# The last tile's steps behind its attended values: other banks, and an earlier place in the order

## The chip, the cores and the metric

One core of a Trainium2 chip runs the whole program. The metric is device time in microseconds (us); 830.11 us is the median of three runs of the kernel before.

## The reference

32 sequences of 128 tokens, 256 features, all in float32. What is computed for each sequence `x` (a "tile" below):

```python
x = x + tanh(g_xattn) * cross_attention(layernorm(x), ctx, mask)        # part "A": 16 heads of 16
y = layernorm(x)
# part "B":
q = k = rope(y) @ Wqk;  v = y @ Wv                                      # 16 heads, causal
u = layernorm(y + softmax(q k^T / 4, causal) v @ Wo; ln1)
gates = top2(softmax(u @ Wg + bg))                                      # 8 experts, two kept
m = u + sum_e gates[e] * (u @ We + be)                                  # all 8 products are computed
x = x + tanh(g_ffn) * layernorm(m; ln2)
```

## The kernel before, in words

There is no loop in the program: five Python functions write out the instruction order of five engines, and semaphores tie them together. `for r in rounds` emits, per round, two tiles; each step is called with its own tile number, `2 * r - 6` for instance, so that up to ten tiles are in flight. A step whose tile is outside 0 to 31 emits nothing (`live`). Each engine runs its own list strictly in the order written; a step that waits holds everything behind it on its engine.

TensorE (`tensor_program`, L385 to L741) makes for a tile: scores, attended values (`attend`, L561), their transposition to rows (`normalise`, L579), the transposes of the normalised values (`o_transposed`), the output product (`project_o`), the transposes of u (`u_transposed`), the gate product (`gate`), the transposes of the gates, the bias product (`expert_bias_sum`, L611) and four products of two experts each (`expert_pair`, L613, six matmuls of 512 columns through `products`, L395). `keep_busy` (L407) emits matmuls of which nobody reads the result; they only occupy TensorE.

Products are made in float32r from a high and a low part of each operand. So a transposed tile in PSUM is read by ScalarE, which writes the high part (`high_part`, L756), and then by VectorE, which subtracts it and writes the low part (`low_part`, L971); TensorE waits for the latter.

VectorE (L928 to L1251) also divides by the softmax sums (`inverse_sums` L1043, `normalise` L1051), adds the residual (`finish_b` L1069), takes mean and variance (`statistics` L952, `mean_variance` L960), applies them (`apply_u`, `apply_v`, L964), computes the gates from L1077 (`gate`, `gate_rank`, `gate_choice`, to L1107), and adds up the experts: `bias_sum` (L1122) and eight `expert_sum` (L1131) for a tile, each reading what the one before wrote. GpSimd takes the roots (`inverse_root`, L1260 and L1263), scales and shifts u (`scale_shift_u`, L1334 and L1336), and finishes the output (`finish`, L1305 to L1311). SyncE loads and stores; `y_out` is one buffer, so `finish` waits for the store before.

PSUM has eight banks. Four are `score_banks`, for the scores of one tile at a time; the table `WORK_USES` deals the other four, `work_banks`, out to everything else in a fixed turn: `work_bank(use, n)` gives the bank, and `work_last(use, n)` finds the use before it in that bank, for whose reader `take_work` makes TensorE wait. For the last tiles:

```python
    ("pair3", 1, 2, 3, (("moe", 9, 9),)),          # odd tiles: work bank 2, read by the last expert sum
    ("B_normalise", 1, 2, 2, (("B_on", 1, 1),)),   # odd tiles: the next use of work bank 2
```

After tile 31's scores (exponentials read for the last time at 791.7 us) the score banks have no further use.

Of the kernel before, what the change touches and what calls it, by code (L numbers as in the profile page):

```python
# [21 lines left out]
GROUPS = HEADS // GROUP  # L22
# [8 lines left out]
PAIR = 2  # L31
# [3 lines left out]
U_SLOTS = 2  # L35
# [100 lines left out]
def build(nc, dram, out):  # L136
    tiles = out.shape[0]
    with ExitStack() as ctx:
# [96 lines left out]
        def live(t):  # L235
            return 0 <= t < tiles

        def work_bank(use, n):

            key = (use, None) if (use, None) in WORK_AT else (use, n % PAIR)  # L240
            return work_banks[WORK_USES[WORK_AT[key]][2]]

        def work_last(use, n):

            key, pair = ((use, None), n) if (use, None) in WORK_AT else ((use, n % PAIR), n // PAIR)
            bank, behind = WORK_USES[WORK_AT[key]][2:4]
            turn = (pair + behind) * len(WORK_USES) + WORK_AT[key] - 1
            while turn >= 0:
                _, half, other_bank, behind, readers = WORK_USES[turn % len(WORK_USES)]
# [134 lines left out]

        def tensor_program(pe):  # L385
            def take_work(use, t):
                for name, value in work_last(use, t):
                    pe.wait_ge(sem[name], value)
                return work_bank(use, t)
# [237 lines left out]
            for r in rounds:  # L627
# [5 lines left out]
                if r == 0:  # L633
                    keep_busy("A_max_t", 0, 6)
                x_t(2 * r)
                project_o("B", 2 * r - 5)
# [5 lines left out]
                expert_pair(0, 2 * r - 6)  # L642
                expert_bias_sum(2 * r - 6)
                expert_pair(1, 2 * r - 6)
                expert_pair(2, 2 * r - 6)
                if r == 1:
                    keep_busy("A_v", 2, 15)
# [4 lines left out]
                rope_transposed(2 * r - 2)  # L652
                subtract_max("A", 2 * r - 1)
                normalise("B", 2 * r - 4)
                expert_pair(3, 2 * r - 6)
# [4 lines left out]
                u_transposed(2 * r - 5)  # L660
                y_transposed(2 * r - 3)
                if r == 2:
                    keep_busy("A_v", 4, 4)
# [36 lines left out]
                if r == 18:  # L700
                    keep_busy("pair1", 31, 3)
                expert_bias_sum(2 * r - 5)
                expert_pair(1, 2 * r - 5)
                if r == 0:
                    keep_busy("A_max_t", 0, 13)
# [1 line left out]
                    keep_busy("rope_t", 1, 14)  # L707
                if r == 2:
                    keep_busy("B_normalise", 1, 8)
                scores_t("A", 2 * r)  # L710
                transpose_max("A", 2 * r)
                rope_transposed(2 * r - 1)
# [1 line left out]
                expert_pair(2, 2 * r - 5)  # L714
                project_k_b(r - 1)
                expert_pair(3, 2 * r - 5)
                project_q_b(r - 1)
                if r == 17:
                    keep_busy("u_t", 30, 5)
                normalise("B", 2 * r - 3)  # L720
                u_transposed(2 * r - 4)
                if r == 1:
                    keep_busy("A_values", 2, 8)
                if r == 2:
# [6 lines left out]
                o_transposed("B", 2 * r - 3)  # L731
                project_v_a(2 * r + 1)
                normalise("A", 2 * r)
                if r == 16:
# [10 lines left out]
        def scalar_program(act):  # L745
# [112 lines left out]
            for r in rounds:  # L858
# [16 lines left out]
                keep_keys("B", r - 4)  # L875
                keep_queries("B", r - 4)
                high_part("y_t", y_t, "y_t", ("B_v_mm", 1), 2 * r - 8)
                high_part("u_t", u_t, "u_t", ("e_mm", 4), 2 * r - 10)
                raw_values("A", 2 * r - 6)
                high_part("B_o_t", o_t["B"], "B_ot", ("B_o_mm", 1), 2 * r - 9)  # L880
                max_transposed("B", 2 * r - 8)
                if r == 3:
                    split_high("Bo")
# [44 lines left out]
        def vector_program(dve):  # L928
# [212 lines left out]
            for r in rounds:  # L1141
# [46 lines left out]
                mean_variance("1", 2 * r - 6)  # L1188
                gates_low(2 * r - 7)
                maxima("A", 2 * r - 2)  # L1190
                bias_sum(2 * r - 7)
                max_parts("A", 2 * r - 2)
                expert_sum(0, 2 * r - 7)
                expert_sum(1, 2 * r - 7)
                expert_sum(2, 2 * r - 7)
# [5 lines left out]
                apply_u(2 * r - 6)  # L1201
                expert_sum(4, 2 * r - 7)
                expert_sum(5, 2 * r - 7)
                expert_sum(6, 2 * r - 7)
# [3 lines left out]
                inverse_sums("B", 2 * r - 5)  # L1208
                normalise("B", 2 * r - 5)
# [12 lines left out]
                low_part("u_t", u_t, "u_t", 2 * r - 6)  # L1222
                apply_v(2 * r - 7)
                low_part("B_o_t", o_t["B"], "B_ot", 2 * r - 5)
                mean_variance("A", 2 * r + 1)
                if r == 1:
                    split_low("Bo")
                low_part("A_o_t", o_t["A"], "A_ot", 2 * r - 2)
                gate(2 * r - 6)
                add_values("B", 2 * r - 4)  # L1230
                finish_a(2 * r - 2)
# [4 lines left out]
                finish_b(2 * r - 5)  # L1236
# [4 lines left out]
                statistics("1", 2 * r - 5)  # L1241
                gates_low(2 * r - 6)
                mean_variance("1", 2 * r - 5)
                apply_y(2 * r - 2)
                maxima("A", 2 * r - 1)
                bias_sum(2 * r - 6)
# [4 lines left out]
                apply_u(2 * r - 5)  # L1251

        def gpsimd_program(pool):
# [133 lines left out]
            for r in rounds:  # L1389
                base_a(2 * r - 5)  # L1390
                inverse_root("2", 2 * r - 10, "vn")
                context_parts(2 * r - 2)
                mask_of_tile(2 * r - 3)
                for g in range(GROUPS):
                    causal(g, 2 * r - 7)
                inverse_root("B", 2 * r - 5, "yn")
                inverse_root("A", 2 * r - 2, "xn")
                rope(2 * r - 5)
                context_parts(2 * r - 1)
                if r == 4:  # L1400
                    fold_gains()
                inverse_root("1", 2 * r - 8, "un")
                finish(2 * r - 10)
                base_b(2 * r - 7)
                scale_shift_u(2 * r - 8)
# [9 lines left out]
                inverse_root("1", 2 * r - 7, "un")  # L1415
                finish(2 * r - 9)
                scale_shift_u(2 * r - 7)
# [55 lines left out]
```

## Time and profile before

| | |
|---|---|
| median of 3 runs (lowest, highest) | 830.11 us (830.05, 830.32) |
| the profiled execution | 831.21 us |
| its span, first to last instruction | 829.5 us |
| TensorE, VectorE, ScalarE, GpSimd busy | 94%, 80%, 68%, 57% of the span |
| mean granted clock of TensorE | 0.994 |

Times in the trace count from the span's start. The profiled execution is one single run; 1.7 us of it lie outside the span. A matmul's busy time overlaps the next one's: back to back, 512 columns issue every 0.23 us but each is shown with 0.39 us. "idle" in a row is the engine's idle time just before it and what ended it.

### The profile page before, as it was taken

How to read it: one execution, taken by the hardware profiler on the slowest of the kernel's cores; microseconds unless marked ns; L12 is line 12 of the kernel's file. 1: busy time of each engine (PE TensorE's matmuls, PEld its weight loads, DVE VectorE, ACT ScalarE, POOL GpSimd, SP SyncE). 2: the span in 40 equal slices, each digit the busy share in tenths (PEclk: the TensorE clock that was granted, in tenths of full speed). 3: DMA queues.
4: the chain of work that ended last, by engine and by line, in shares of the span. 5: the costliest groups of instructions: out<-in, count | busy, mean ns of one | idle time of the engine just before them, and what ended most of it. 6: DMA issues, size and time to landing. Idle time of an engine off the chain costs nothing.

```text
span 829.5 us, 24325 instructions
## 1 busy us (share of the span) xinstructions
PE 779.7 (94%) x9515; PEld 611.9 (74%) x9515; DVE 667.5 (80%) x1908; ACT 564.4 (68%) x1268; POOL 473.0 (57%) x854
## 2 busy tenths in 40 slices
PE   8888989999999999999999999999999999999896
PEld 4465768777787787778787788778778777777663
DVE  5756668797978979797988979797988979787876
ACT  5786767777786777777776777678677777764320
POOL 8434535566665646566574646566564655555343
PEclk9999999999999999999999999999999999999999
DMA  7510000010100101010100101010010000000000
GB/s 202 159 39 16 2 17 16 8 37 9 37 8 2 37 8 36 9 36 9 29 16 2 38 8 37 8 37 9 10 35 2 9 8 8 9 8 8 8 7 20
DMA packets 33570, 20.75 MB, mean 25 GB/s; under 512 B 11672, under 2 KB 33456, under 8 KB 33456
## 3 DMA queue, kind: packets, MB, share of 16 engines
q1 hardware_dynamic: 33456, 19.19, 8.1%
q8 instruction: 76, 1.25, 0.6%
q14 instruction: 38, 0.31, 0.1%
HBM read 14.99 MB, written 4.19 MB: 23 GB/s over the span
## 4 chain that ended last, share of the span: by engine, by line
PE 56%; ACT 24%; DVE 14%; issue 4%; POOL 1%; DMA 0%; SPq 0%; DVEq 0%; POOLq 0%
PE bank L395 26%; PE bank L516 8%; PE bank L535 7%; ACT bank L776 6%; DVE neg_max_A L1022 6%; ACT bank L785 5%; DVE moe L1131 4%; ACT probs_B L826 3%; PE bank L556 3%; PE bank L585 3%; ACT probs_A L826 3%; PE bank L574 2%; PE bank L404 2%; ACT k_heads_B L809 2%; PE bank L546 1%
## 5 line engine op out<-in xcount | busy, mean ns | idle before, releaser
L1343 POOL TENSOR_SCALAR_AFFINE_SELECT probs_B<-probs_B 128x512 f32<-128x512 f32 x128 | 77.3, 640 | 184.4 <-ACT probs_B L826 184.4
L1131 DVE SCALAR_TENSOR_TENSOR moe<-bank,gates,moe 128x256 f32<-128x256 f32 x256 | 123.2, 481 | 48.2 <-PE bank L395 33.2
L785 ACT ACTIVATE bank<-mask_add 128x512 f32<-128x512 bf16 x128 | 76.6, 602 | 49.2 <-DVE neg_max_A L1022 49.2
L395 PE MATMUL bank<-w_expertsa,u_t_a 128*128 128x512 f32 x256 | 105.6, 413 | 0.1
L395 PE MATMUL bank<-w_expertsa,u_t_b 128*128 128x512 f32 x256 | 100.9, 394 | 0.0
L395 PE MATMUL bank<-w_expertsb,u_t_a 128*128 128x512 f32 x256 | 100.9, 394 | 0.0
L1022 DVE TENSOR_REDUCE neg_max_A<-bank 128x4 f32<-128x512 f32 x128 | 79.5, 684 | 11.9 <-PE bank L516 11.5
L1022 DVE TENSOR_REDUCE neg_max_B<-bank 128x4 f32<-128x512 f32 x128 | 79.3, 682 | 5.5 <-PE bank L516 5.5
L776 ACT ACTIVATE bank<-mask_add 128x512 f32<-128x512 bf16 x128 | 69.8, 626 | 0.0
L776 ACT ACTIVATE bank<-causal_add 128x512 f32<-128x512 bf16 x128 | 69.7, 623 | 0.0
L826 ACT ACTIVATE probs_A<-bank 128x512 f32<-128x512 f32 x128 | 66.1, 603 | 4.4 <-PE bank L556 2.2
L826 ACT ACTIVATE probs_B<-bank 128x512 f32<-128x512 f32 x128 | 66.2, 607 | 3.2 <-PE bank L556 1.1
L834 ACT ACTIVATE o_raw<-bank 128x512 f32<-128x512 f32 x64 | 38.5, 602 | 27.8 <-PE bank L574 27.8
L395 PEld LDWEIGHTS bank<-w_expertsa,u_t_a 128*128 128x128 f32 x256 | 49.1, 192 | 10.6 <-issue 0.4
L1260 POOL TENSOR_SCALAR var_eps<-mean_var 128x1 f32<-128x1 f32 x64 | 12.3, 192 | 77.7 <-DVE mean_var L960 75.2
L395 PEld LDWEIGHTS bank<-w_expertsa,u_t_b 128*128 128x128 f32 x256 | 48.1, 188 | 11.4
L395 PEld LDWEIGHTS bank<-w_expertsb,u_t_a 128*128 128x128 f32 x256 | 48.3, 189 | 6.7
L535 PEld LDWEIGHTS bank<-q_heads_A,k_heads_A 32*128 32x128 f32 x1024 | 31.4, 186 | 22.4 <-ACT bank L785 22.4
L809 ACT ACTIVATE k_heads_A<-bank,k_cols_A,head_rows 128x256 f32<-128x256 f32 x64 | 30.9, 565 | 23.0 <-PE bank L395 23.0
L535 PE MATMUL bank<-q_heads_A,k_heads_A 32*128 32x128 f32 x1024 | 37.5, 283 | 8.1 <-ACT bank L785 7.4
L411 PE MATMUL bank<-ident_bf 128*128 128x512 bf16 x167 | 42.7, 396 | 1.9 <-ACT k_heads_B L809 1.9
L516 PE MATMUL bank<-k_heads_A,q_heads_A 32*128 32x256 f32 x512 | 36.7, 399 | 5.8 <-ACT bank L776 4.7
(224 smaller groups left out, 2440.5 us busy)
## 6 DMA issues: line engine op xcount, KB each, us to landing
x_in<-in_x SPq DMA_DIRECT2D x32, 128.0 KB, 2.2
ctx_t<-in_ctxT SPq DMA_DIRECT2D x32, 128.0 KB, 2.2
out<-y_out SPq DMA_DIRECT2D x32, 128.0 KB, 1.7
w_stage<-in_expertsT SPq DMA_DIRECT2D x8, 256.0 KB, 4.3
mask_u<-in_masks SPq DMA_DIRECT2D x32, 32.0 KB, 2.1
w_stage<-in_in_projT SPq DMA_DIRECT2D x3, 256.0 KB, 4.8
w_stage<-in_WkT SPq DMA_DIRECT2D x1, 256.0 KB, 3.5
w_stage<-in_WvT SPq DMA_DIRECT2D x1, 256.0 KB, 3.6
```

Of the source, the lines that this page charges most:

```text
L395: done = pe.matmul(out_ap, l, r, start=n == 0, stop=n == len(terms) - 1)
L411: pe.matmul(bank[:], ident_bf[:], ident_bf[:].unsqueeze(1).to_broadcast([P, GROUP, P]), start=True, stop=True)
L516: done = pe.matmul(score_banks[g][:, c * 2 * P:(c + 1) * 2 * P], queries[strip, half, c, :], keys[strip, half, c, :, :], start=False, stop ...
L535: pe.matmul(score_banks[g][:, i * P:(i + 1) * P], keys[strip, half, c, odd, :], queries[strip, half, c, :], start=tag == "B" and i == 0, s ...
L776: act.activation(score_banks[g][:].rearrange("p (h k) -> p h k", k=P), mask[:, 0:1, :].to_broadcast([P, GROUP, P]), ACT.Copy).then_inc(sem ...
L785: act.activation(score_banks[g][:].rearrange("p (h k) -> p h k", k=P), mask_add[t % MASK_SLOTS][:, 1:2, :].to_broadcast([P, GROUP, P]), AC ...
L809: act.activation(k_heads[tag][pair % PAIR_SLOTS][:, :, c, odd, :], bank[:, c * PAIR * P:(c + 1) * PAIR * P].rearrange("p (j n) -> p j n", ...
L826: act.activation(probs[tag][:, g * GROUP:(g + 1) * GROUP, :].rearrange("p h q -> p (h q)"), score_banks[g][:], ACT.Exp, scale=SCALE).then_ ...
L834: act.activation(o_raw[:], work_bank(tag + "_values", t)[:], ACT.Copy).then_inc(sem[tag + "_or"], 1)
L1022: dve.tensor_reduce(neg_max[tag][:, g * GROUP:(g + 1) * GROUP], score_banks[g][:].rearrange("p (h k) -> p h k", k=P), AXIS_X, ALU.max, neg ...
L1131: dve.scalar_tensor_tensor(out=moe[(e + 1) % 2][:], in0=bank[:, (e % 2) * EMBED:(e % 2 + 1) * EMBED], scalar=gates[:, e:e + 1], in1=moe[e ...
L1343: pool.affine_select(out=part, in_=part, compare_op=ALU.is_ge, fill=0.0, base=0, pattern=[[0, GROUP], [1, P]], channel_multiplier=-1).then ...
```

## The change

Six uses of the last tiles are taken out of the fixed turn and given a score bank each (`LATE`: bank, and the semaphore and value for which `take_work` waits). Then steps of tiles 29 to 31 change places, in round 17 or 18 on TensorE, 18 on VectorE, 19 on GpSimd and 20 on ScalarE. Behind tile 31's `attend`, the two orders on TensorE are (k(n) is `keep_busy` with n matmuls):

```
before: bias29 pair1,2,3(29) k(5) normalise31 u_t30 o_t31 | gate30 out31 k(4) gates_t30 pair0(30) bias30 pair1,2,3(30) u_t31 k(8) gate31 pair0(31) gates_t31 k(3) bias31 pair1,2,3(31)
after:  bias29 normalise31 pair1(29) o_t31 pair2,3(29) u_t30 out31 | gate30 pair0,1(30) gates_t30 bias30 pair2(30) u_t31 pair3(30) k(6) gate31 pair0(31) gates_t31 k(3) bias31 pair1,2,3(31)
```

On VectorE, from the low part of tile 29's gates on (s0 to s7 are the expert sums, `low` the low parts, `stat` is statistics and mean):

```
before: bias29 s0-s3(29) apply_u30 s4-s7(29) stat2(29) inverse,normalise31 low_u30 apply_v29 low_o31 gate30 rank,choice30 finish_b31 stat1(31) bias30 s0-s2(30) apply_u31 s3-s7(30) stat2(30) low_u31 gate31 ...
after:  apply_u30 bias29 s0,s1(29) inverse,normalise31 s2,s3(29) low_o31 s4,s5(29) low_u30 s6,s7(29) stat2(29) apply_v29 finish_b31 stat1(31) gate30 rank,choice30 apply_u31 bias30 s0-s7(30) stat2(30) low_u31 gate31 ...
```

(In the order before, the low part of tile 30's gates lies between the two halves of stat1(31); after, it follows apply_u31.) ScalarE writes the high part of `o_t` 31 ahead of that of `u_t` 30. GpSimd does `scale_shift_u` 30 and 31 ahead of `finish` 28 and 29. `u_transposed` no longer takes its work bank's wait, for any tile; instead ScalarE waits for the products that read the old u before it writes that of tiles 30 and 31. The core of the diff:

```diff
+        LATE = {("B_normalise", tiles - 1): (0, "B_exp", GROUPS * tiles), ("B_o_t", tiles - 1): (1, "B_exp", GROUPS * tiles),
+                ("B_out", tiles - 1): (2, "B_exp", GROUPS * tiles), ("pair3", tiles - 3): (3, "B_exp", GROUPS * tiles),
+                ("u_t", tiles - 1): (0, "B_on", tiles), ("gate", tiles - 1): (1, "B_ot_b", tiles)}
         def work_bank(use, n):
+            if (use, n) in LATE:
+                return score_banks[LATE[use, n][0]]
...
-                if other_bank == bank and live(PAIR * pair):
+                if other_bank == bank and live(PAIR * pair) and (half is None or (other, PAIR * pair + half) not in LATE):
...
             def take_work(use, t):
+                if (use, t) in LATE:
+                    pe.wait_ge(sem[LATE[use, t][1]], LATE[use, t][2])
+                    return work_bank(use, t)
...
-                transpose_two(take_work("u_t", t), u[t % U_SLOTS], "u_t", t)
+                transpose_two(work_bank("u_t", t), u[t % U_SLOTS], "u_t", t)
...
-                if r == 18:
-                    keep_busy("gates_t", 30, 4)
+                if r == 18:
+                    expert_pair(0, 2 * r - 6)
+                if r == 18:
+                    expert_pair(1, 2 * r - 6)
                 transpose_gates(2 * r - 6)
...
-                    keep_busy("pair0", 31, 8)
+                    keep_busy("pair0", 31, 6)
...
+                if r == 17:
+                    normalise("B", 2 * r - 3)
                 expert_pair(1, 2 * r - 5)
...
-                if r == 17:
-                    keep_busy("u_t", 30, 5)
...
+                if use == "u_t" and t >= tiles - 2:
+                    act.wait_ge(sem[read[0]], read[1] * t)
                 act.activation(dst[0][:], work_bank(use, t)[:, 0:EMBED], ACT.Copy).then_inc(sem[name + "_a"], 1)
```

## Rows read from the trace of the kernel before

**Rows 1.** The page: busy time by engine, and one expert matmul (mean ns).
```profile
PE 779.7 (94%) x9515; PEld 611.9 (74%) x9515; DVE 667.5 (80%) x1908; ACT 564.4 (68%) x1268; POOL 473.0 (57%) x854
...
L395 PE MATMUL bank<-w_expertsa,u_t_b 128*128 128x512 f32 x256 | 100.9, 394 | 0.0
```
**Rows 2.** Busy time by stretch: PE, PEld, DVE, ACT, POOL, then PEclk, DMA share, GB/s.
```profile
800.00:802.00 2.00, 1.40 (x11) 0.93 (x8) 1.55 (x6) 0.77 (x2) 0.75 (x2) 1.00 0.00 0
...
803.00:804.00 1.00, 1.00 (x5) 0.72 (x5) 0.90 (x6) 0.25 (x2) 0.00 (x0) 0.50 0.00 0
...
806.00:807.00 1.00, 1.00 (x6) 0.80 (x5) 0.47 (x2) 0.11 (x1) 0.19 (x1) 0.94 0.00 0
```
**Rows 3.** The chain that ended last, 793 to 830 us: start, us, what.
```profile
800.56 0.43 DVE o_norm_B L1051
...
811.70 0.04 issue
...
818.01 4.22 PE bank L395 x18
```
**Rows 4.** Timeline of VectorE: start, us, engine, line, operation [idle before, releaser].
```profile
794.20 0.42 DVE L1122 TENSOR_TENSOR moe<-bank,u 128x256 f32<-128x256 f32 x1 [0.73 <-PE bank L611]
...
799.95 0.18 DVE L960 BATCH_NORM_AGGREGATE mean_var<-stats 128x2 f32<-128x6 f32 x1
800.27 0.26 DVE L1043 RECIPROCAL inv_sum_B<-bank 128x16 f32<-128x16 f32 x1
...
802.27 0.16 DVE L1077 TENSOR_TENSOR logits<-bank,gate_bias 128x8 f32<-128x8 f32 x1
...
804.10 0.23 DVE L1107 TENSOR_SCALAR gates<-chosen,gate_inv 128x24 f32<-128x24 f32 x1
804.25 0.41 DVE L1069 TENSOR_TENSOR u_n<-bank,base_B 128x256 f32<-128x256 f32 x1
...
807.54 0.42 DVE L1122 TENSOR_TENSOR moe<-bank,u 128x256 f32<-128x256 f32 x1 [0.90 <-PE bank L611]
...
809.64 0.41 DVE L964 TENSOR_SCALAR u_n<-u_n,mean_var,rstd 128x256 f32<-128x256 f32 x1
809.97 2.83 DVE L1131 SCALAR_TENSOR_TENSOR moe<-bank,gates,moe 128x256 f32<-128x256 f32 x5
...
813.39 0.39 DVE L971 TENSOR_TENSOR u_t_b<-bank,u_t_a 128x256 fp32r<-128x256 f32 x1
814.49 0.17 DVE L1077 TENSOR_TENSOR logits<-bank,gate_bias 128x8 f32<-128x8 f32 x1 [0.70 <-PE bank L595]
```
**Rows 5.** Timeline of TensorE.
```profile
793.78 0.38 PE L611 MATMUL bank<-expert_bias,gates_t 128*128 128x256 f32 x1
...
799.60 0.63 PE L585 MATMUL bank<-ident,o_raw 128*128 128x128 f32 x4 [0.16 <-DVE moe L1131]
...
803.65 1.93 PE L411 MATMUL bank<-ident_bf 128*128 128x512 bf16 x4
...
816.61 0.33 PE L604 MATMUL bank<-ident,gates 128*128 128x128 f32 x1 [0.67 <-DVE gates L1107]
...
817.63 0.39 PE L611 MATMUL bank<-expert_bias,gates_t 128*128 128x256 f32 x1
```
**Rows 6.** Timeline of ScalarE.
```profile
793.92 0.60 ACT L834 ACTIVATE o_raw<-bank 128x512 f32<-128x512 f32 x1 [0.76 <-PE bank L574]
800.49 0.38 ACT L756 ACTIVATE u_t_a<-bank 128x256 fp32r<-128x256 f32 x1 [5.97 <-PE bank L405]
```
**Rows 7.** Timeline of GpSimd.
```profile
793.18 0.55 POOL L1263 TENSOR_TENSOR rstd<-var_eps,neg_half 128x1 f32<-128x1 f32 x1
...
800.50 0.56 POOL L1263 TENSOR_TENSOR rstd<-var_eps,neg_half 128x1 f32<-128x1 f32 x1
...
810.13 0.74 POOL L1334 TENSOR_TENSOR u_n<-u_n,row_ln_w 128x256 f32<-128x256 f32 x1 [0.35 <-DVE u_n L964]
810.95 0.74 POOL L1336 TENSOR_TENSOR u<-u_n,row_ln_b 128x256 f32<-128x256 f32 x1
```

More of the change, by code:

```diff
@@ L248, in work_last @@
             while turn >= 0:
-                _, half, other_bank, behind, readers = WORK_USES[turn % len(WORK_USES)]
+                other, half, other_bank, behind, readers = WORK_USES[turn % len(WORK_USES)]
                 pair = turn // len(WORK_USES) - behind
-                if other_bank == bank and live(PAIR * pair):
+                if other_bank == bank and live(PAIR * pair) and (half is None or (other, PAIR * pair + half) not in LATE):
                     m = pair if half is None else PAIR * pair + half
@@ L635, in tensor_program @@
                 x_t(2 * r)
-                project_o("B", 2 * r - 5)
+                if r != 18:
+                    project_o("B", 2 * r - 5)
                 attend("B", 2 * r - 4)
@@ L659, in tensor_program @@
                 attend("A", 2 * r - 1)
-                u_transposed(2 * r - 5)
+                if r != 18:
+                    u_transposed(2 * r - 5)
                 y_transposed(2 * r - 3)
@@ L709, in tensor_program @@
                     keep_busy("B_normalise", 1, 8)
+                if r == 17:
+                    o_transposed("B", 2 * r - 3)
                 scores_t("A", 2 * r)
@@ L716, in tensor_program @@
                 expert_pair(3, 2 * r - 5)
+                if r == 17:
+                    u_transposed(2 * r - 4)
+                if r == 17:
+                    project_o("B", 2 * r - 3)
                 project_q_b(r - 1)
-                if r == 17:
-                    keep_busy("u_t", 30, 5)
-                normalise("B", 2 * r - 3)
-                u_transposed(2 * r - 4)
+                if r != 17:
+                    normalise("B", 2 * r - 3)
+                if r != 17:
+                    u_transposed(2 * r - 4)
                 if r == 1:
@@ L730, in tensor_program @@
                 attend("A", 2 * r)
-                o_transposed("B", 2 * r - 3)
+                if r != 17:
+                    o_transposed("B", 2 * r - 3)
                 project_v_a(2 * r + 1)
@@ L877, in scalar_program @@
                 high_part("y_t", y_t, "y_t", ("B_v_mm", 1), 2 * r - 8)
+                if r == 20:
+                    high_part("B_o_t", o_t["B"], "B_ot", ("B_o_mm", 1), 2 * r - 9)
                 high_part("u_t", u_t, "u_t", ("e_mm", 4), 2 * r - 10)
                 raw_values("A", 2 * r - 6)
-                high_part("B_o_t", o_t["B"], "B_ot", ("B_o_mm", 1), 2 * r - 9)
+                if r != 20:
+                    high_part("B_o_t", o_t["B"], "B_ot", ("B_o_mm", 1), 2 * r - 9)
                 max_transposed("B", 2 * r - 8)
@@ L1190, in vector_program @@
                 maxima("A", 2 * r - 2)
+                if r == 18:
+                    apply_u(2 * r - 6)
                 bias_sum(2 * r - 7)
@@ L1194, in vector_program @@
                 expert_sum(1, 2 * r - 7)
+                if r == 18:
+                    inverse_sums("B", 2 * r - 5)
+                if r == 18:
+                    normalise("B", 2 * r - 5)
                 expert_sum(2, 2 * r - 7)
@@ L1200, in vector_program @@
                 low_part_of_pair("rope_t", rope_t, "rope_t", 2 * r - 3)
-                apply_u(2 * r - 6)
+                if r != 18:
+                    apply_u(2 * r - 6)
+                if r == 18:
+                    low_part("B_o_t", o_t["B"], "B_ot", 2 * r - 5)
                 expert_sum(4, 2 * r - 7)
                 expert_sum(5, 2 * r - 7)
+                if r == 18:
+                    low_part("u_t", u_t, "u_t", 2 * r - 6)
                 expert_sum(6, 2 * r - 7)
@@ L1207, in vector_program @@
                 mean_variance("2", 2 * r - 7)
-                inverse_sums("B", 2 * r - 5)
-                normalise("B", 2 * r - 5)
+                if r != 18:
+                    inverse_sums("B", 2 * r - 5)
+                if r != 18:
+                    normalise("B", 2 * r - 5)
                 low_part("y_t", y_t, "y_t", 2 * r - 4)
@@ L1221, in vector_program @@
                 apply_x(2 * r)
-                low_part("u_t", u_t, "u_t", 2 * r - 6)
+                if r != 18:
+                    low_part("u_t", u_t, "u_t", 2 * r - 6)
                 apply_v(2 * r - 7)
-                low_part("B_o_t", o_t["B"], "B_ot", 2 * r - 5)
+                if r != 18:
+                    low_part("B_o_t", o_t["B"], "B_ot", 2 * r - 5)
                 mean_variance("A", 2 * r + 1)
@@ L1228, in vector_program @@
                 low_part("A_o_t", o_t["A"], "A_ot", 2 * r - 2)
+                if r == 18:
+                    finish_b(2 * r - 5)
+                if r == 18:
+                    statistics("1", 2 * r - 5)
+                if r == 18:
+                    mean_variance("1", 2 * r - 5)
                 gate(2 * r - 6)
@@ L1235, in vector_program @@
                 gate_choice(2 * r - 6)
-                finish_b(2 * r - 5)
+                if r != 18:
+                    finish_b(2 * r - 5)
                 if r == 0:
@@ L1240, in vector_program @@
                 low_part_of_pair("x_t", xn_t, "xn", 2 * r)
-                statistics("1", 2 * r - 5)
+                if r != 18:
+                    statistics("1", 2 * r - 5)
+                if r == 18:
+                    apply_u(2 * r - 5)
                 gates_low(2 * r - 6)
-                mean_variance("1", 2 * r - 5)
+                if r != 18:
+                    mean_variance("1", 2 * r - 5)
                 apply_y(2 * r - 2)
@@ L1250, in vector_program @@
                 expert_sum(2, 2 * r - 6)
-                apply_u(2 * r - 5)
+                if r != 18:
+                    apply_u(2 * r - 5)
         def gpsimd_program(pool):
@@ L1402, in gpsimd_program @@
                 inverse_root("1", 2 * r - 8, "un")
+                if r == 19:
+                    scale_shift_u(2 * r - 8)
                 finish(2 * r - 10)
                 base_b(2 * r - 7)
-                scale_shift_u(2 * r - 8)
+                if r != 19:
+                    scale_shift_u(2 * r - 8)
                 base_a(2 * r - 4)
@@ L1415, in gpsimd_program @@
                 inverse_root("1", 2 * r - 7, "un")
+                if r == 19:
+                    scale_shift_u(2 * r - 7)
                 finish(2 * r - 9)
-                scale_shift_u(2 * r - 7)
+                if r != 19:
+                    scale_shift_u(2 * r - 7)
                 if r == 1:
```

7 lines of the change are left out of this document (5 added, 2 removed).

## The prediction

> **What bounds the kernel now.** I read the busy shares first [rows 1]: TensorE is busy 94% of the span, VectorE 80%. The edits that move work act only on tiles 29 to 31, so only the last 36 us matter. The table by stage [rows 2] shows that TensorE's share there is no measure of need: from before 803 until after 806 us its granted clock is at the lower of its two levels (1.2 GHz, 0.50 in the table), and part of its busy time is filler (L411, `keep_busy`: 5, 4, 8 and 3 matmuls in this stretch). The chain of waits [rows 3] then shows what sets the end: tile 31's values normalised on VectorE, filler, tile 31's u finished by GpSimd at 811.7 [rows 7], eight fillers, the gate, and 18 expert matmuls up to 822.23. From there to the end nothing of the change acts: 7.3 us of fixed tail. So the question is at what time VectorE starts tile 31's gate (now 814.49 [rows 4]); every 0.1 us there is 0.1 us at the end, as long as TensorE has pair 0 of tile 31 ready by the time the gates are.
>
> The timelines [rows 4 to 7] show that VectorE's own queue is nearly as long as the stage. One expert sum takes 0.57 us in a chain (2.83 us for 5 [rows 4]), eight of them with the bias sum 5.0 us, and three tiles' sums are still to come at 794 us: some 15 us. Gate, ranks and choice take 2.06 us per tile (802.27 to 804.10+0.23 [rows 4]), twice here, and the rest (normalising, low parts, statistics, applying) about 6 us. That is 25 us of queue between 793.8 and the last sum's end at 823.3, which are 29.5 us. The most that any order could win is thus some 4.5 us, and it is lost by every wait that the new order puts in front of VectorE.
>
> **Part 1: the banks.** With work bank 2, tile 31's TensorE normalise had to wait for tile 29's last expert sum: it starts at 799.60 [rows 5]. In a score bank it needs only the raw values: ScalarE has them at 793.92+0.60 = 794.52 [rows 6], so it starts at 794.57, 5.0 us earlier. The `u_t` work wait that goes for all tiles costs nothing now: TensorE's order, which has waited for later VectorE work by then, implies it. By the nearest rows, bounded by the 0.04 us steps called issue [rows 3] for 32 tiles if each were exposed, it lies between 0 and -1.3 us; I take 0, since the timeline shows no gap ahead of u's transposes that it could fill. The new ScalarE wait for `e_mm` is met before the transposed tile is there (0 us) for tile 30; for tile 31 it moves the high part of u behind pair 3 of tile 30, costed below.
>
> **Part 2: tile 29's sums with tile 31's steps between them.** I follow both queues on the clock of the profiled run. TensorE: bias product of tile 29 at 793.78 as before [rows 5], normalise 794.57 to 795.04 (0.63 busy [rows 5], the last 0.16 beside the next), pair 1 of tile 29 until 796.44 (18 expert matmuls take 4.22 us [rows 3], so a pair of six 1.40; one alone is shown 0.39 long [rows 1], so its result comes 0.16 after the next could issue). VectorE: apply u of tile 30 needs the root of tile 30, 793.18+0.55 = 793.73 [rows 7], and runs at 793.83 in 0.33; bias sum 794.20 as before [rows 4]; two sums until 795.71; inverse sums and normalise (0.29 + 0.42; the reciprocal starts at 800.27 [rows 4], the product at 800.56 [rows 3]) until 796.42. TensorE's transposes of it at 796.50 with almost no stall, pair 2 until 798.16 (1.66 for both), pair 3 until 799.56. VectorE: sums 2 and 3 from 796.63 to 797.70, low part of tile 31's values, sums 4 and 5 from 798.35 to 799.42. Here comes the first new wait: next in VectorE's queue is the low part of tile 30's u, whose transposes TensorE issues only after pair 3, at 799.61. ScalarE takes 0.38 for the high part [rows 6], so the low part starts at 800.49: **1.07 us idle**, with sums 6 and 7 ready from 799.75 but queued behind. They run from 800.83 to 801.90, then statistics until 802.58.
>
> The second new wait: next is apply v of tile 29, which wants GpSimd's root of that variance. Before, tile 31's normalising and u's low part lay between. The way there took from 799.95+0.18 = 800.13 to 800.50+0.56 = 801.06 [rows 4, 7], and a crossing between the two engines 0.08 (809.64+0.41 to 810.13 [rows 4, 7]): **1.0 us idle**, apply v at 803.6. Who waits behind both: gate of tile 30, through it TensorE's gate transposes, and all of tile 30's sums. Then the moved finish B, statistics and mean of tile 31, 1.0 us (0.41 for finish B [rows 4], 0.6 for statistics and mean, as between the last sum's end at 812.80 and 813.39), so the gate starts at 804.96 rather than 802.27, and tile 30's gates are there at 804.96+2.06 = 807.02. The moved GpSimd steps are hidden: scale and shift takes 1.56 (810.13 to 811.69 [rows 7]), for tile 30 now from 794.3, and pushes the finish of tile 28 and its store 2 us back. On SyncE's queue only stores are left by then, and y_out is next rewritten after 808.9; base B of tile 31 ends by 798.8, 5 us before VectorE wants it.
>
> **Part 3: TensorE meanwhile.** Transposes of u 799.61, output product of tile 31 until 800.7, gate 800.96 to 801.42, pairs 0 and 1 of tile 30 until 804.29. Then it has nothing for 2.8 us, until 807.07. Before, these transposes issued about 805.4 (803.65 and four times 0.43), not at 804.33 when the gates were there, since four fillers at the low clock (1.93 us busy, one each 0.43 [rows 5]) stood in front. Return of the gates to the bias product: 1.02 (816.61 to 817.63 [rows 5]), so 808.10; bias sum 0.41 later at 808.51. Before it started at 807.54 [rows 4]. **The order costs 0.97 us there.** From the bias sum: 0.53 + 8 x 0.57 = about 5.0, end of tile 30's sums 813.5 against 812.80; the difference shrinks by the 0.33 of apply u, which lay among those sums (809.64 to 809.97 [rows 4]) and now runs at 806.94. Its u is there at 808.98 instead of 811.70, 2.7 us sooner; but u's low part still stands behind the statistics of tile 30 (0.59 after the last sum), at 814.10 instead of 813.39. So the earlier u is worth nothing: VectorE's queue ends last. Then 1.10 us to the gate on VectorE, as from 813.39 to 814.49 before [rows 4]: 815.20. **Sum: 815.20 - 814.49 = +0.7 us**, TensorE at full clock.
>
> The fillers: the 5 and 4 that go are under the moved work, so they are no gain of their own, and their cover, the clock, is priced here. 2.8 us without a matmul, then 0.7 more around the gates, is longer than what stood before the fall in the profiled run (1.40 us of work in 800 to 802 [rows 2]); so I expect the lower level once after 806. If it spans the gates' return, the transpose and the bias product at the half rate take some 0.1 and 0.2 more (a 512-column matmul goes from 0.23 to the fillers' 0.43 at it): +0.3. Pair 2 runs until 809.72 and pair 3, behind u's transposes, until 811.43; the sums that read them start at 811.3 and 812.4, so they have 1.4 and 0.8 us of slack, and nothing more is lost. At the least 0 (no fall); at the most, both pairs wholly cold (0.43 a matmul as the fillers [rows 5], so 2.6 a pair): 1.2 + 1.2 + 0.3 - 0.8 = 1.9. I take 0.3. The 8 fillers that become 6 stand before 814.5 and are over by 813: 0.
>
> **Total: +0.7 + 0.3 = +1.0 us.** The profiled execution took 831.21 (span 829.5 and 1.7 around it), 1.1 above the median of the runs; I put the difference on the median: 830.11 + 1.0 = 831.1.
>
> The Trainium skill (TensorE: Matmul & The Clock Gate, Terms) prices a low stretch at its length times one minus the granted share. For the stretch in rows 2, at least 3.1 us, that is 1.6 us, where the trace shows about 1.0 us of lateness on the path (gates ready 804.33, transposed 805.4). By that rule the sum here would be 0.7 + 1.6 = +2.3, 832.4.
>
> **Rivals.** (a) *The cold return.* The clock falls about when the gates come back, or stays low through both products of tile 30, and pair 3 ends after its sum wants it: +0.7 + 1.9 = +2.6, 832.7. For it: nothing fills the 2.8 us, and the filler of 4 that stood there is gone. Against it: the slack of 0.8 to 1.4 us, and the seen low stretch ended after about 3 us. It decides from 1.7 us of loss in total. The skill's rule above is this rival in other words and gives nearly its number; the chance covers both. (b) *VectorE does not stall.* If the products of tile 29 land earlier or the two waits of 1.07 and 1.03 overlap with something, the gates of tile 30 come 2.1 us sooner: 0.7 - 2.1 = -1.4, 828.7. It becomes a gain from the point where TensorE's gate transposes of tile 30 start before about 806.1, a microsecond ahead of the 807.07 above. For it: the queue has 4.5 us of air. Against: both waits follow from the written order, and neither depends on a close race. (c) *It changes nothing.* The gates' later arrival is just balanced by the filler no longer in front and by the removed work waits: 0, 830.1.
>
> **How the numbers follow.** What a measurement here can tell from no change is 0.2%, 1.7 us: faster is below 828.4, slower above 831.8. Forecast 831.1 with its own range 830.3 to 832.0: 0.48. (a) 0.23, (b) 0.15, (c) 0.14. (a) and a tenth of the forecast's spread make slower 0.29; (b) at 828.7 lies just inside the bound; if it comes, more of the 4.5 us of air than its two waits may go with it, so I count most of it as faster: 0.14 with a little unseen. The rest, 0.57, is within. Range: up to (a)'s 832.7, and down to 828.6, which keeps (b)'s own value and leaves out what may come beyond it.
>
> **What would show it.** In the new trace: TensorE's transposes of tile 31's raw values at 794.6 with the raw values as releaser; VectorE idle about 1 us before the low part of tile 30's u and again about 1 us before apply v of tile 29, released by ScalarE and GpSimd; gates of tile 30 near 807.0; TensorE idle 2.5 to 2.8 us before them, and the granted clock down once after it; tile 31's u ready near 809.0 and not waited for; its gate on VectorE at 815.2 to 815.5. I am wrong if the idle time before either of VectorE's two steps is under 0.5 us, if the clock stays low over both products of tile 30, or if anything before 793 us moves.

## The result, and the profile after

The changed kernel takes 832.58 us (median of 7 runs, 831.30 to 833.47) against 830.11 us before: ratio 1.0031, 95% interval 1.0021 to 1.0040. It is slower by 2.5 us. The forecast was +1.0 us, 831.1. 832.58 lies outside the forecast's own range (830.3 to 832.0) and above the 831.8 from which it called a result slower; it lies in the stated range only as rival (a) does, the cold return (832.7).

Of the page of the changed kernel, first the lines that answer to [rows 1]: the shares are the same, so they say nothing about the loss.

```profile
PE 777.1 (94%) x9504; PEld 610.9 (74%) x9504; DVE 667.5 (80%) x1908; ACT 564.2 (68%) x1268; POOL 472.0 (57%) x854
...
L405 PE MATMUL bank<-w_expertsa,u_t_b 128*128 128x512 f32 x256 | 101.6, 397 | 0.0
```

The two profiled executions cannot be compared by their spans (829.5 and 830.6), because the one before had lost 1.1 us earlier on, near 750 us, where TensorE's granted clock was low. These two rows are from the table by stretch of the kernel before (PE, PEld, DVE, ACT, POOL busy, then the granted clock):

```profile
745.00:750.00 5.00, 3.55 (x51) 2.81 (x43) 4.79 (x18) 0.71 (x3) 0.00 (x0) 0.81 0.00 0
750.00:755.00 5.00, 5.00 (x45) 3.97 (x44) 3.08 (x11) 2.73 (x6) 3.16 (x6) 0.85 0.01 3
```

The same stretches of the changed kernel, which issues the same work there:

```profile
745.00:750.00 5.00, 3.54 (x64) 2.61 (x61) 4.79 (x18) 1.39 (x6) 0.00 (x0) 1.00 0.00 0
750.00:755.00 5.00, 4.71 (x57) 3.92 (x56) 4.36 (x15) 2.46 (x6) 3.75 (x7) 1.00 0.01 3
```

With the clock at 1.00 there, the changed kernel starts tile 31's attended values at 791.62, the one before at 792.77. So I measure one length in every kernel, called **the stage** below: from the start of tile 31's attended values on TensorE to the start of its gate on VectorE. Before, it is 814.49 - 792.77 = 21.72 us, after 815.58 - 791.62 = 23.96: **+2.24 us**, beside 2.47 between the medians.

VectorE's timeline of the changed kernel, against [rows 4]:

```profile
793.05 0.42 DVE L1155 TENSOR_TENSOR moe<-bank,u 128x256 f32<-128x256 f32 x1
...
799.23 0.42 DVE L1004 TENSOR_TENSOR u_t_b<-bank,u_t_a 128x256 fp32r<-128x256 f32 x1 [0.96 <-ACT u_t_a L786]
...
802.34 0.41 DVE L997 TENSOR_SCALAR v_n<-moe,mean_var,rstd 128x256 f32<-128x256 f32 x1 [1.03 <-POOL rstd L1323]
...
805.49 0.23 DVE L1140 TENSOR_SCALAR gates<-chosen,gate_inv 128x24 f32<-128x24 f32 x1
...
807.55 0.42 DVE L1155 TENSOR_TENSOR moe<-bank,u 128x256 f32<-128x256 f32 x1 [0.67 <-PE bank L621]
808.08 3.43 DVE L1164 SCALAR_TENSOR_TENSOR moe<-bank,gates,moe 128x256 f32<-128x256 f32 x6
812.82 1.07 DVE L1164 SCALAR_TENSOR_TENSOR moe<-bank,gates,moe 128x256 f32<-128x256 f32 x2 [1.30 <-PE bank L405]
...
814.49 0.39 DVE L1004 TENSOR_TENSOR u_t_b<-bank,u_t_a 128x256 fp32r<-128x256 f32 x1
815.58 0.17 DVE L1110 TENSOR_TENSOR logits<-bank,gate_bias 128x8 f32<-128x8 f32 x1 [0.70 <-PE bank L605]
```

Read the brackets: 0.96 us idle until ScalarE's high part of tile 30's u, 1.03 us until GpSimd's root, and, not forecast, 1.30 us until TensorE's last expert product of tile 30, with tile 31's u ready since 807.65. TensorE's timeline shows why, against [rows 5]:

```profile
793.42 0.66 PE L595 MATMUL bank<-ident,o_raw 128*128 128x128 f32 x4 [0.40 <-ACT o_raw L864]
...
805.78 0.47 PE L614 MATMUL bank<-ident,gates 128*128 128x128 f32 x1 [2.55 <-DVE gates L1140]
806.93 0.58 PE L621 MATMUL bank<-expert_bias,gates_t 128*128 128x256 f32 x1 [0.69 <-DVE gates_t L1148]
...
809.45 0.63 PE L405 MATMUL bank<-w_expertsa,u_t_b 128*128 128x512 f32 x1
...
812.62 1.47 PE L421 MATMUL bank<-ident_bf 128*128 128x512 bf16 x6
```

It stands for 2.55 us before the gate transposes. Then an expert matmul is 0.63 long instead of 0.39, through both products behind the return of the gates. The chain of waits (start, us, what) has both products in a row, pair 2 and pair 3, each now on the path that sets the end (before, no product of tile 30 had held a sum back):

```profile
807.52 2.56 PE bank L405 x6
810.08 0.21 PE bank L414
810.29 0.21 PE bank L415
810.50 2.29 PE bank L405 x6
```

And the table by stretch, against [rows 2], shows the clock from the pause on:

```profile
804.00:805.00 1.00, 0.00 (x0) 0.00 (x0) 0.89 (x6) 0.39 (x2) 0.67 (x2) 1.00 0.00 0
805.00:806.00 1.00, 0.22 (x1) 0.18 (x1) 0.94 (x5) 0.00 (x0) 0.00 (x0) 0.74 0.00 0
806.00:807.00 1.00, 0.32 (x2) 0.07 (x1) 0.32 (x2) 0.28 (x1) 0.81 (x2) 0.50 0.00 0
...
811.00:812.00 1.00, 1.00 (x3) 0.72 (x3) 0.48 (x1) 0.00 (x0) 0.00 (x0) 0.50 0.10 34
812.00:813.00 1.00, 1.00 (x5) 0.54 (x4) 0.18 (x1) 0.13 (x1) 0.00 (x0) 0.85 0.00 0
```

By these rows the granted clock is at the lower level from about 805.5 (0.74 over that microsecond) to about 812.3 (0.85): 6.8 us, where the low stretch of the kernel before, from about 802.7 to 806.1, lasted 3.4.

### The profile page after: what moved, and what is told of

Its sections match the earlier page's. It is cut to its first block, busy times and chain, and to the rows that moved or that the text cites. A ratio compares the mean times of both kernels' runs of the same rounds, so it can differ in the third digit from the quotient of the medians.

```text
span 830.6 us, 24273 instructions
## 1 busy us (share of the span) xinstructions
PE 777.1 (94%) x9504; PEld 610.9 (74%) x9504; DVE 667.5 (80%) x1908; ACT 564.2 (68%) x1268; POOL 472.0 (57%) x854
## 4 chain that ended last, share of the span: by engine, by line
PE 55%; ACT 24%; DVE 14%; issue 4%; POOL 1%; SPq 1%; DMA 0%; DVEq 0%; POOLq 0%
PE bank L405 26%; PE bank L526 8%; PE bank L545 7%; ACT bank L806 6%; DVE neg_max_A L1055 6%; ACT bank L815 5%; DVE moe L1164 4%; ACT probs_B L856 3%; PE bank L595 3%; PE bank L566 3%; ACT probs_A L856 3%; PE bank L584 2%; PE bank L414 2%; ACT k_heads_B L839 2%; PE bank L556 1%
## 5 line engine op out<-in xcount | busy, mean ns | idle before, releaser
L421 PE MATMUL bank<-ident_bf 128*128 128x512 bf16 x156 | 39.1, 390 | 1.9 <-ACT k_heads_B L839 1.9
```

The source lines that it names most:

```text
L421: pe.matmul(bank[:], ident_bf[:], ident_bf[:].unsqueeze(1).to_broadcast([P, GROUP, P]), start=True, stop=True)
```

## The experiments

Theory 1: the loss is +0.7 us of waits in VectorE's queue plus 1.5 us of TensorE at its lower clock behind the pause that those waits make. Rivals: the clock is hidden beside VectorE; VectorE is bound by its amount of work, so waits only move; the banks or the waits taken out cost by themselves. Each kernel was timed in five rounds beside the kernel before, and the ratio is to that kernel (830.11 us with the first result, 829.79 to 830.05 in these).

| | ratio (95% interval) | median us | stage in its trace, us |
|---|---|---|---|
| before | | 830.11 | 21.72 |
| after | 1.0031 (1.0021 to 1.0040) | 832.58 | 23.96 |
| after_again | 1.0037 (1.0024 to 1.0049) | 833.02 | 23.85 |
| fill11 | 1.0023 (1.0014 to 1.0031) | 831.48 | 22.42 |
| fill4 | 1.0019 (1.0009 to 1.0029) | 831.17 | 22.40 |
| fill_both | 1.0017 (1.0008 to 1.0026) | 831.72 | 22.42 |
| only_v | 0.9999 (0.9989 to 1.0009) | 829.54 | 21.15 |
| only_u | 1.0003 (0.9994 to 1.0012) | 829.77 | 21.62 |
| no_stalls | 0.9999 (0.9990 to 1.0009) | 828.94 | 20.20 |
| no_stalls_k14 | 0.9982 (0.9973 to 0.9991) | 828.70 | 20.21 |
| early_gates | 0.9991 (0.9981 to 1.0000) | 829.05 | 20.55 |
| banks_alone | 0.9998 (0.9988 to 1.0008) | 829.68 | 21.46 |
| before_warm | 0.9991 (0.9982 to 1.0000) | 829.89 | 20.61 |

**The yardstick, and the pause filled.**

> The changed kernel once more, as the yardstick beside the variants. It ran at 1.0031 (1.0021 to 1.0040) of the kernel before. Both theories expect the same again: ratio 1.002 to 1.004, 832 to 833 us where the kernel before has 830.1; in the trace the chain from tile 31's attended values to its gate on VectorE near 22.9 us at a cold return of the clock (20.7 before).

It repeated. (The 22.9 and 20.7 us of that expectation count from about 1 us later, where tile 29's bias product stands: 792.63 and 793.78.)

```diff
 # fill11: TensorE, round 18, behind expert_pair(1, 30), ahead of transpose_gates(30)
+                if r == 18:
+                    keep_busy("gates_t", 30, 11)
```

> The changed kernel with 11 matmuls of filler before the gate transposes of tile 30, where TensorE stands 2.55 us without work. Theory 1 (the loss is +0.7 us of waits in VectorE's queue and +1.5 us of TensorE at its lower clock behind that pause): the granted clock stays at 1.00 through tile 30's products, VectorE's 1.30 us wait before the expert sum of pair 3 goes, and the time falls 1.5 us below the changed kernel's, to a ratio of 1.0009 (830.8). Theory 2 (the late gates and the queue are the loss, and the lower clock is hidden beside VectorE): no difference to the changed kernel, 1.003 (832.6). If the filler itself comes late into the path, up to 0.3 us more than theory 1.

The stage went from 23.96 to 22.42, by the 1.54 us of theory 1, and the median fell by 1.54 us against after_again (by the two ratios it is 1.2). TensorE's rows of this kernel, the filler and the gate transposes behind it:

```profile
802.86 2.55 PE L421 MATMUL bank<-ident_bf 128*128 128x512 bf16 x11
805.59 0.33 PE L614 MATMUL bank<-ident,gates 128*128 128x128 f32 x1 [0.18 <-DVE gates L1142]
```

The ratio, however, is 1.0023 and not 1.0009. The clock fell all the same, later, at 814.0, behind a pause of 1.88 us before tile 31's gate. By stretch, fill11:

```profile
812.00:815.00 3.00, 1.81 (x8) 1.58 (x9) 2.09 (x11) 0.39 (x2) 1.44 (x3) 0.83 0.00 0
815.00:818.00 3.00, 3.00 (x10) 1.75 (x10) 1.63 (x8) 0.28 (x1) 1.45 (x2) 0.60 0.00 0
```

**The second pause filled too, and less in the first.**

```diff
 # fill_both: as fill11, and
-                    keep_busy("pair0", 31, 6)
+                    keep_busy("pair0", 31, 14)
```

> The changed kernel with both of TensorE's pauses filled: 11 matmuls before tile 30's gate transposes, and 14 rather than 6 before tile 31's gate. With the first alone the fall of the clock moved from 806 to 813 us, and the time was 1.0023 of the kernel before. Theory 1: with both, no fall before 824 us, what is left is the order's own loss, and the time falls by another 0.5 to 1.0 us, to a ratio of 1.0010 to 1.0017. Theory 2: the rest is not the clock's, ratio 1.0023.

The clock held at 1.00 until 824 us in its trace, and the way from tile 31's gate to its bias sum is back to 3.57 us (fill11 3.97). The ratio, 1.0017, is at the upper edge of theory 1 and its interval overlaps that of fill11, so the timing alone does not separate them.

> The changed kernel with the 4 matmuls of filler, which the change took away there, put back ahead of tile 30's gate transposes; 11 held the clock at that place. They leave 1.7 us of pause, and 0.7 more behind the transposes. Theory 1 (what counts is how much of the stretch TensorE works): the clock falls all the same, once, later or for a shorter time than the 6.4 us of the changed kernel; 22.9 to 23.9 us from the attended values to the gate, 1.0025 to 1.0033 of the kernel before. If the four were all that the change lacked, 22.4 us and 1.0023.

This one went against me in the trace: the clock stayed at 1.00 in the profiled execution, with 1.67 us of pause left, and the stage is 22.40. Its 12 runs spread from 830.41 to 834.08, wider than any other kernel's. The three slowest (832.45 and more) have a mean granted clock of 0.992 to 0.993 where the profiled one has 0.996, so they may have had the fall; no trace shows one. What part of 11 is needed stays open.

**VectorE's two steps put back.**

```diff
 # no_stalls: VectorE, round 18
-                if r == 18:
-                    low_part("u_t", u_t, "u_t", 2 * r - 6)
                 expert_sum(6, 2 * r - 7)
                 expert_sum(7, 2 * r - 7)
+                if r == 18:
+                    low_part("u_t", u_t, "u_t", 2 * r - 6)
...
-                apply_v(2 * r - 7)
+                if r != 18:
+                    apply_v(2 * r - 7)
...
                 gate_choice(2 * r - 6)
+                if r == 18:
+                    apply_v(2 * r - 7)
```

> The changed kernel with two of VectorE's steps put further back in round 18: the low part of tile 30's u behind expert sums 6 and 7 of tile 29, and apply v of tile 29 behind the gates of tile 30. No filler is added. Theory 1 (both queue waits are real and the pause of TensorE is their consequence): the two waits of 0.96 and 1.03 us shrink to under 0.3, tile 30's gates come 2.2 us earlier, TensorE's pause before their transposes falls from 2.55 to about 0.3 us, the clock doesn't fall there, and the time is 1.5 us below the kernel BEFORE (0.7 - 2.2), ratio 0.998; with a fall of the clock later, behind the six fillers, up to 0.9990. Theory 2 (VectorE is bound by its amount of work, the waits only show where the air is): the waits turn up elsewhere in its queue and the time stays within 0.5 us of the changed kernel, 1.003.

With no matmul of filler added, the pause and with it the early fall went: the median is 828.94 us against 833.02 for after_again. That is 4.1 us less between medians and 3.2 by the two ratios; in the traces the stage is 3.65 us shorter, at 20.20. Waits of that size did not turn up elsewhere. VectorE's rows in this kernel, with 0.31 where 0.96 was, and none at apply v:

```profile
798.47 1.07 DVE L1164 SCALAR_TENSOR_TENSOR moe<-bank,gates,moe 128x256 f32<-128x256 f32 x2 [0.31 <-PE bank L405]
799.46 0.41 DVE L1004 TENSOR_TENSOR u_t_b<-bank,u_t_a 128x256 fp32r<-128x256 f32 x1
...
803.14 0.23 DVE L1140 TENSOR_SCALAR gates<-chosen,gate_inv 128x24 f32<-128x24 f32 x1
803.30 0.40 DVE L997 TENSOR_SCALAR v_n<-moe,mean_var,rstd 128x256 f32<-128x256 f32 x1
```

That is the whole difference between slower and no slower. The ratio of 0.9999 is a miss all the same: I had 0.998, or up to 0.9990 with a later fall. A later fall is in the trace, at 812.2, behind a pause of 1.87 us before tile 31's gate; the transposes of tile 31's gates and the three fillers behind them ran at half rate:

```profile
811.04 0.28 PE L605 MATMUL bank<-w_gate,u_t_a 128*128 128x16 f32 x1 [1.87 <-DVE u_t_b L1004]
...
814.08 1.49 PE L421 MATMUL bank<-ident_bf 128*128 128x512 bf16 x3
```

```diff
 # no_stalls_k14: as no_stalls, and
-                    keep_busy("pair0", 31, 6)
+                    keep_busy("pair0", 31, 14)
```

> The changed kernel with VectorE's two steps put further back, and now 14 rather than 6 matmuls of filler before tile 31's gate. Without the filler the clock fell at 812 us, in TensorE's pause of 1.9 us, and the ratio was 0.9999 (0.9990 to 1.0009). Theory 1: the clock holds, tile 31's bias sum comes 0.4 us sooner behind its gates and the products behind it run at full rate: 0.5 to 0.8 us less, ratio 0.9992. If the gain of the order is fully there, 0.9985. Theory 2: 0.9999.

The clock held from 800 to 821 us, tile 31's bias sum follows its gate by 3.56 us (4.11 in no_stalls), and the ratio is 0.9982 (0.9973 to 0.9991): faster than both kernels, 1.35 us under the median of the one before. The later fall is worth those 0.55 us in the traces; the two ratios lie further apart, with intervals that just overlap. It was timed once, on one chip. By stretch:

```profile
809.00:812.00 3.00, 3.00 (x14) 1.18 (x12) 2.62 (x7) 0.38 (x1) 0.10 (x1) 1.00 0.12 44
812.00:815.00 3.00, 2.17 (x12) 1.55 (x12) 2.09 (x13) 0.39 (x2) 1.34 (x3) 1.00 0.00 0
```

**Each step alone**, with 7 and 14 matmuls of filler in the two pauses, so that the clock stays up in the stage:

> The changed kernel with both pauses of TensorE filled (7 and 14 matmuls), and apply v of tile 29 alone put behind tile 30's gates. From the start of tile 31's attended values to its gate on VectorE the changed kernel takes 23.96 us, 22.42 with filled pauses, 20.2 with both steps put back. Theory 1 (the two waits add up, 1.03 for this one): tile 30's gates 1.0 us sooner, and about 21.4 us here. Theory 2 (one wait hides the other): 22.4 or 20.2. Time: 1.0007 of the kernel before.

> The same with the low part of tile 30's u alone put behind sums 6 and 7 of tile 29. Theory 1: the wait of 0.96 us shrinks to 0.3 and the two sums run in it, so the gates come 0.7 to 1.1 us sooner, about 21.5 us from the attended values to the gate. Theory 2: 22.4 or 20.2. Time: 1.0008 of the kernel before.

The ratios, 0.9999 and 1.0003, are a little under the 1.0007 and 1.0008 that I had; the traces are what tells the steps apart. Against 22.42 of fill_both: apply v alone 1.27 us, the low part alone 0.80, together 2.07, where both at once (no_stalls_k14) bring 2.21. So they add up but for 0.14 us. Apply v alone brings more than its wait of 1.03, because its own 0.33 us also leaves the way to the gates. It would bring more still: tile 30's gates are ready 1.48 us sooner than in fill_both, at 805.23, but the last of the 7 fillers is still in front, and their transposes start at 805.56.

**The finish of tile 31 put back as well.**

```diff
 # early_gates: as no_stalls_k14, and on VectorE, round 18
-                if r == 18:
-                    finish_b(2 * r - 5)
-                if r == 18:
-                    statistics("1", 2 * r - 5)
-                if r == 18:
-                    mean_variance("1", 2 * r - 5)
                 gate(2 * r - 6)
...
                 gate_choice(2 * r - 6)
+                if r == 18:
+                    finish_b(2 * r - 5)
+                if r == 18:
+                    statistics("1", 2 * r - 5)
+                if r == 18:
+                    mean_variance("1", 2 * r - 5)
...
-                if r == 18:
-                    apply_u(2 * r - 5)
                 gates_low(2 * r - 6)
+                if r == 18:
+                    apply_u(2 * r - 5)
```

> As the one before it, and also tile 31's finish B, statistics and mean go back behind tile 30's gates, and apply u of tile 31 goes behind the low part of tile 30's gates, so that it lies beside the bias product. Theory 1 (VectorE's queue up to the gates of tile 30 sets the stage): those gates come 1.0 us sooner; TensorE, which has two expert products to finish first, can use 0.5 of it, and the ratio is 0.0006 under the one before it, 0.9985. If the later u of tile 31 or a filler takes its place, the same as the one before it.

A miss. The gates of tile 30 do come 0.73 us earlier, but apply u then waits 0.40 us for the root, with the bias sum behind it, which starts 0.27 us later than in no_stalls_k14. (TensorE also waits 0.65 us for tile 31's u, but VectorE has no wait from the bias sum to the low part of that u, so this costs nothing.) Stage 20.55 against 20.21: by the traces the change's place for these steps is the better one. The ratios, 0.9991 and 0.9982, have intervals that overlap.

```profile
804.72 0.41 DVE L997 TENSOR_SCALAR u_n<-u_n,mean_var,rstd 128x256 f32<-128x256 f32 x1 [0.40 <-POOL rstd L1326]
```

**The banks alone, in the old order**: `LATE`, its lookups and ScalarE's wait, and no work wait before u's transposes, as in the diff ahead; none of the moves.

> The kernel before with the score banks (LATE), the work wait of u's transposes taken out and the new wait on ScalarE, in the OLD order of steps and with all the old fillers. Theory 1: the banks by themselves are worth the 0.16 us that TensorE waited before its normalise of tile 31, and the 32 removed waits nothing: ratio 0.9995 to 1.0003. Theory 3 (the banks or the removed and added waits cost or gain by themselves): a ratio clear of 1, towards 1.003 if they are the loss, or 0.9985 if the 32 removed waits are worth 0.04 us each.

Nothing: 0.9998. Banks and removed waits cost nothing and gain nothing measurable; it is the order that loses.

**The kernel before, with its own fall of the clock filled.**

```diff
 # before_warm: TensorE, rounds 17 and 18
+                if r == 17:
+                    keep_busy("B_o_t", 31, 3)
                 o_transposed("B", 2 * r - 3)
...
+                if r == 18:
+                    keep_busy("B_out", 31, 2)
                 project_o("B", 2 * r - 5)
```

> The kernel before with 5 more matmuls of filler in TensorE's two pauses in front of the fall of its clock at 802.7 us: 3 ahead of the transposes of tile 31's values, 2 ahead of tile 31's output product. Theory 1 (a low stretch in this stage costs about 1.0 us of path wherever it stands): the clock stays up from 800 to 806, tile 30's gates are transposed at once, the bias sum of tile 30 comes 1.0 us after the return of its gates and not 3.2, and the time is 0.5 to 1.1 us below the kernel before, ratio 0.9990. Theory 2 (the clock's fall is hidden beside VectorE): ratio 1.000.

The clock held at 1.00 and the stage shrank from 21.72 to 20.61, by 1.11 us; the ratio is 0.9991. VectorE had its gates at 803.96 and TensorE transposed them at 804.02:

```profile
803.73 0.23 DVE L1111 TENSOR_SCALAR gates<-chosen,gate_inv 128x24 f32<-128x24 f32 x1
...
804.02 0.33 PE L604 MATMUL bank<-ident,gates 128*128 128x128 f32 x1
```

So the order by itself, both kernels at full clock, costs 22.42 - 20.61 = 1.8 us; against the profiled execution of the kernel before it is 0.7, because that one had lost 1.1 to its own fall. The same yardstick cuts the gain of no_stalls_k14: 20.61 - 20.21 = 0.4 us is what the order is worth without its two waits, and the other 1.1 of its 1.51 us came from keeping the clock up, which five fillers do in the old order as well.

## Why the prediction was right or wrong

**Banks (Part 1): right.** The normalise starts on its raw values, 1.80 us after the attended values began (I had 794.57 - 792.77 = 1.80). The banks alone are worth 0.02% with an interval of 0.1% on either side.

**VectorE's two waits (Part 2): right in place, releaser and size.** 0.96 and 1.03 us idle against 1.07 and 1.0 forecast; gates of tile 30 ready 14.10 us after the attended values began, against 807.02 - 792.77 = 14.25. What each costs alone, and that they add up, is shown by only_v, only_u and no_stalls.

**The sum at full clock, +0.7: right, with some luck.** fill_both has TensorE at full clock throughout the stage, and its stage is 22.42 against 21.72: +0.70. But tile 30's bias sum is +0.83 late in it (15.60 us after the attended values, 14.77 before) and not +0.97, and from there to the gate only 0.13 came back (6.82 against 6.95) and not 0.26: two misses of the same size cancel.

**The price of the clock, +0.3: wrong, and the term that failed.** The +0.3 for the return of the gates came out (the bias sum is 15.93 us after the attended values, 15.60 in fill_both). What failed is the step behind it, "1.4 and 0.8 us of slack, and nothing more is lost". I expected "the lower level once after 806", over the gates' return only. It stayed low for 6.8 us, through nearly all of both products. They took 2.56 and 2.29 us instead of 1.40, and the slack of 0.8 was overrun by 1.30 us, which is VectorE's wait before sum 6. Measured: 23.96 - 22.42 = 1.54 us. With it my own sum would have been 0.7 + 1.54 = +2.24, 832.35. By the forecast's own sign of being wrong ("if the clock stays low over both products of tile 30") its mechanism was wrong: the stated range holds the result only because it reached up to rival (a). I had the mechanism as rival (a), at 1.9 for both pairs wholly cold, and gave it 0.23: I took the one low stretch in the trace as the length of every one. This one came with a pause of 2.55 us, where the longest of the short ones around the fall that I had read was 0.59. Fill11 shows that the fall comes of the pause: 11 matmuls whose result nobody reads take off the 1.54. Why this stretch was twice as long as the others no run shows.

**What a low stretch costs.** The 6.8 us low in this trace cost the stage 1.54 us, and the 3.4 us in that of the kernel before 1.11 (before_warm). The Trainium skill (TensorE: Matmul & The Clock Gate, Terms) would price them at half their length, 3.4 and 1.7 us. Neither run agrees: part of the slowed work lies beside VectorE's queue, and in the kernel before four fillers are part of it. The rule's total of +2.3 in the forecast was near the result only because I had put a stretch of 3.1 us into it.

**Fillers, 8 to 6 at no cost: right in the changed kernel's trace, not in every kernel.** There the clock held at that place. Once the earlier pause was filled or gone, the fall came there (fill11, no_stalls), and 14 instead of 6 took no_stalls from 0.9999 to 0.9982.

**Rival (b)**, the stage without VectorE's stalls, was priced at -1.4 us; no_stalls_k14 has 20.21 - 21.72 = -1.51 and is 1.4 us under the kernel before. It was not what the change does, but the price was right against that execution. **Rival (c)** is out, by the interval.

**Where I put the difference.** The profiled execution of the kernel before had two falls of the clock, each worth 1.1 us, and ran 1.1 above the median. I scaled nothing for that, and it is not typical. In the 28 runs timed with after_again, 10 lie at 828.7 to 828.9 with a mean granted clock of 0.997 or 0.998, 14 from 829.7 to 830.7 with 0.995 to 0.997, and four at 830.9 and above with 0.994, as the profiled one has. That points to no, one and two falls, but only the last kind was traced. Against a run without a fall in the stage the order loses 1.8 us and not 0.7. fill_both fits that: its 1.0017 is 1.4 us, where the stages alone give 0.7, and its fastest run (830.61) is 1.9 above the fastest of the kernel before beside it (828.72). Between medians the loss was 2.47, and 2.24 between the traces.

## What to carry to other kernels

When steps are moved up on an engine that works strictly in order, go through the waits of each moved step in the new place: each of the two steps here waited about 1 us in front of ready work and cost 0.80 and 1.27 us, though the engine's total is unchanged. Putting two such steps back behind the ready work turned 1.0037 into 0.9999. And where fillers are taken out and leave a new pause of TensorE, price the work behind it at half rate, and allow for a low stretch longer than the last one you saw. Before a gain is put down to an order, compare both orders with the clock kept up: of 1.51 us here 0.4 were the order's.

## What the runs showed of the hardware

The granted clock fell behind quite different pauses: 1.27 us in one piece near 747 us (kernel before), two short ones near 801 (0.59 and 0.41 us), 1.87 us before tile 31's gate (no_stalls). The products behind the first, in the trace before, where the clock fell, and in the one after, where it held:

```profile
747.85 1.93 PE L535 MATMUL bank<-q_heads_B,k_heads_B 32*128 32x128 f32 x32 [1.27 <-DVE neg_max_B L1022]
```

```profile
747.75 1.17 PE L545 MATMUL bank<-q_heads_B,k_heads_B 32*128 32x128 f32 x32 [1.27 <-DVE neg_max_B L1055]
```

The work around 747 is the same in every kernel, yet the clock fell there in the traces of before, after_again, fill4, only_v, no_stalls_k14 and banks_alone and not in the other seven; and a pause of 1.89 us before tile 31's gate in fill4 had no fall. So one identical stretch of instructions comes out 1.1 us longer in one execution than in another, and a single trace does not tell a kernel's typical number of falls. The traces of fill4 and before_warm also start the first attended values at 71.41 and 71.48 us, the others at 70.7 to 71.0, and stay late by that; the cause is open, and it is one more reason not to compare the spans of single executions. A low stretch lasted 3.4 us (before, 802.7 to 806.1) or twice that (after, 805.5 to 812.3).
